# GNN layer, one core: z ahead of n on TensorE and ScalarE, DMA issues apart, edge bias added by VectorE

## The reference

```
h    = relu(layernorm(x))
hid  = relu([h[src], h[dst]] @ W1[t] + b1[t])        # t = type of the edge
m    = hid @ W2[t] + b2[t]
agg  = segment_sum(m, dst)
gi, gh = agg @ W_ih.T + b_ih, h @ W_hh.T + b_hh      # r, z, n parts
r, z = sigmoid(i_r + h_r), sigmoid(i_z + h_z)
n    = tanh(i_n + r * h_n)
out  = x + (1 - z) * n + z * h
```

## Time and profile before

| | |
|---|---|
| median of 3 runs | 1838.65 us (1838.35 to 1839.18) |
| profiled execution | 1840.2 us, its span 1838.3 us |
| TensorE busy | 1667.1 us, 91% |
| VectorE busy | 1595.2 us, 87% |
| ScalarE busy | 1494.6 us, 81% |
| GpSimd busy | 1178.9 us, 64% |
| DMA | 319.72 MB, mean 174 GB/s |

### The profile page before, as it was taken

The page is one execution under the profiler, slowest core; times in us unless marked ns, Lnnn a source line. Parts: engine busy times, 40 slices in busy tenths (PEclk is TensorE's granted clock), DMA queues, the critical chain, the costliest instruction groups (busy, mean ns, idle before and its releaser), DMA issues.

```text
span 1838.3 us, 43100 instructions
## 1 busy us (share of the span) xinstructions
PE 1667.1 (91%) x10182; PEld 1416.6 (77%) x10182; DVE 1595.2 (87%) x4186; ACT 1494.6 (81%) x3401; POOL 1178.9 (64%) x1982
## 2 busy tenths in 40 slices
PE   0226799999999999999999999999999999999998
PEld 0125688888888888888888888888888888888787
DVE  8597798989888988898889888989899989898776
ACT  0025789889888898898888888889898889888795
POOL 5777777776776777777765656666666566666310
PEclk9999899999999999999999999999999999999999
DMA  2225677777777776777677777777777777777653
GB/s 70 51 48 139 168 195 194 192 192 192 198 187 193 191 194 186 187 192 191 187 193 187 190 188 187 187 190 189 189 190 188 190 186 192 189 187 191 161 136 100
DMA packets 477071, 319.72 MB, mean 174 GB/s; under 512 B 106705, under 2 KB 463009, under 8 KB 476962
## 3 DMA queue, kind: packets, MB, share of 16 engines
q10 hardware_dynamic: 261792, 156.12, 28.6%
q1 hardware_dynamic: 185730, 106.99, 25.3%
q0 software_dynamic: 29440, 55.47, 11.8%
HBM read 211.65 MB, written 106.72 MB: 173 GB/s over the span
## 4 chain that ended last, share of the span: by engine, by line
PE 73%; ACT 8%; issue 4%; ACTq 3%; DVE 2%; DMA 0%; SPq 0%; POOL 0%; DVEq 0%; POOLq 0%
PE bank L1329 16%; PE bank L1331 12%; PE bank L1330 12%; PE bank L1409 10%; PE bank L1399 5%; PE bank L1391 5%; PE bank L1421 3%; PE bank L1420 3%; PE bank L1437 3%; ACT n_h L1194 3%; PE bank L1447 3%; ACT n_zc L1282 2%; ACTq L1211 2%; ACT e_r L1270 2%; ACTq L1232 2%
## 5 line engine op out<-in xcount | busy, mean ns | idle before, releaser
L580 POOL DMA_INDIRECT e_x<-in_x,rows_now x816 | 799.6, 980 | 241.7 <-issue 233.4
L1177 ACT ACTIVATE e_h<-e_x,shift,rstd 128x128 f32<-128x128 f32 x816 | 355.3, 493 | 93.6 <-DVE shift L1048 93.6
L1194 ACT ACTIVATE n_h<-n_x,shift,rstd 128x128 f32<-128x128 f32 x784 | 362.8, 489 | 2.1 <-issue 2.1
L1329 PE MATMUL bank<-n_h_hi,whh_hi 128*128 128x512 f32 x588 | 263.0, 447 | 25.3 <-ACT n_zc L1282 18.3
L1113 DVE TENSOR_TENSOR n_d<-bank,n_n 128x512 f32<-128x512 f32 x196 | 135.5, 691 | 160.7 <-ACT n_n L1278 149.1
L1329 PE MATMUL bank<-n_a_hi,wih_hi 128*128 128x512 f32 x588 | 249.3, 424 | 0.9 <-DVE bank L1083 0.9
L1071 DVE TENSOR_SCALAR n_sel<-iota,n_rel 128x256 fp32r<-128x256 f32 x784 | 237.8, 365 | 8.6 <-POOL n_rel L631 7.2
L1409 PE MATMUL bank<-n_sel,n_win 128*128 128x256 f32 x1568 | 234.9, 292 | 8.6 <-DVE n_sel L1071 8.4
L1331 PE MATMUL bank<-n_h_hi,whh_lo 128*128 128x512 f32 x588 | 232.9, 396 | 0.0
L1330 PE MATMUL bank<-n_h_lo,whh_hi 128*128 128x512 f32 x588 | 232.7, 396 | 0.0
L1331 PE MATMUL bank<-n_a_hi,wih_lo 128*128 128x512 f32 x588 | 232.3, 395 | 0.0
(11 more groups left out here) (179 smaller groups left out, 3895.4 us busy)
## 6 DMA issues: line engine op xcount, KB each, us to landing
n_win<-messages SPq DMA_DIRECT2D x1568, 64.2 KB
messages<-e_msg ACTq DMA_DIRECT2D x204, 257.0 KB, 2.7
n_x<-in_x ACTq DMA_DIRECT2D x195, 256.0 KB
out<-n_out ACTq DMA_DIRECT2D x195, 256.0 KB
e_x<-in_x,rows_now POOLq DMA_INDIRECT x816
rows_now<-lists SPq DMA_DIRECT2D x204, 2.0 KB
lists<-picks,list_rows POOLq DMA_INDIRECT x72
w<-in_W SPq DMA_DIRECT2D x1, 512.0 KB, 4.5
```

Of the source, the lines that this page charges most:

```text
L580: G.indirect_dma_start(e_x[:, s, 2 * end + t, :], None, x, bass.IndirectOffsetOnAxis(ap=rows_now[:, s, t, end:end + 1], axis=0)).then_inc( ...
L1177: last = A.activation(e_h[:, s % 2, k, :], e_x[:, s, k, :], ACT.Relu, scale=rstd[:, slot, col + k:col + k + 1], bias=shift[:, slot, col + ...
L1194: last = A.activation(n_h[:, s % 2, cols], n_x[:, s, cols], ACT.Relu, scale=rstd[:, slot, col + 4 + k:col + 5 + k], bias=shift[:, slot, co ...
L1329: T.matmul(o, w_hi, v_hi, start=start, stop=False, skip_group_check=onto)
```

## The change

TensorE makes the z gate ahead of the i_n gate. ScalarE follows: n_zc comes ahead of n_n, and its n_h pieces and DMA issues are put in other places: the store of messages ahead of the last two e_h, one n_h between n_h_hi and n_a_hi, the store of out ahead of an n_h and e_r, the load of x between n_zc and an n_h. The second edge bias is no longer a product of TensorE. VectorE adds it: e_m (SBUF) = messages (PSUM) + b2_all, where b2_all is filled once by ScalarE from a product of TensorE at the start. High and low parts of the messages are then taken from e_m, and TensorE's hidden layer of the next unit waits for e_biased instead of e_low.

```diff
@@ vector, step
                     V.tensor_tensor(e_msg[:, s, :, D:2 * D],
-                                    bank[BE1][:, message_part].rearrange("p (t d) -> p t d", t=2),
+                                    e_m[:].rearrange("p (t d) -> p t d", t=2),
                                     e_msg[:, s, :, 0:D].bitcast(F32), ALU.subtract).then_inc(e_low, 1)
...
                 ln_part(i, m, 5)
+                q = i - 9
+                if within(q, UNITS):
+                    dve.wait_ge(e_messaged, q + 1)
+                    if isinstance(q, int) and q == 0:
+                        dve.wait_ge(b2_copied, 1)
+                    if due(q):
+                        dve.wait_ge(e_low, q)
+                    first = 2 * ((m - 9) % 2)
+                    V.tensor_tensor(e_m[:], bank[BE1][:, message_part], b2_all[:, first * D:(first + 2) * D],
+                                    ALU.add).then_inc(e_biased, 1)
@@ scalar, step
-                normalise_edges(i, m, (0, 1, 2))
+                normalise_edges(i, m, (0, 1))
...
-                normalise_edges(i, m, (3,))
                 store_messages(i, m)
+                normalise_edges(i, m, (2, 3))
...
                     if due(g - 1):
-                        act.wait_ge(n_gate_z, g - 1)
+                        act.wait_ge(n_gate_in, g - 1)
                     A.activation(n_h_hi[:, s, :], bank[BT[s]][:], ACT.Copy).then_inc(n_hhi, 1)
+                normalise_nodes(i, m, (0,))
+                if within(g, NG):
                     act.wait_ge(n_summed, g + 1)
                     A.activation(n_a_hi[:, s, :], bank[BA][:], ACT.Copy).then_inc(n_ahi, 1)
-                normalise_nodes(i, m, (0,))
                 store_out(i, m)
-                load_x(i, m)
+                normalise_nodes(i, m, (1,))
...
-                normalise_nodes(i, m, (1, 2))
...
-                    act.wait_ge(n_gate_in, g + 1)
-                    if due(g - 1):
-                        act.wait_ge(n_ded, g - 1)
-                    A.activation(n_n[:, s, :], bank[BIN][:], ACT.Tanh, bias=bih[:, 2:3]).then_inc(n_ned, 1)
                     act.wait_ge(n_gate_z, g + 1)
                     if due(g - 1):
                         act.wait_ge(n_eed, g - 1)
                     A.activation(n_zc[:, s, :], bank[BRZ][:], ACT.Sigmoid, bias=bneg[:, 1:2],
                                  scale=-1.0).then_inc(n_zed, 1)
+                load_x(i, m)
+                normalise_nodes(i, m, (2,))
+                if within(g, NG):
+                    act.wait_ge(n_gate_in, g + 1)
+                    if due(g - 1):
+                        act.wait_ge(n_ded, g - 1)
+                    A.activation(n_n[:, s, :], bank[BIN][:], ACT.Tanh, bias=bih[:, 2:3]).then_inc(n_ned, 1)
@@ tensor, step
-                        pe.wait_ge(e_low, q)
+                        pe.wait_ge(e_biased, q)
...
+                    pe.wait_ge(n_red, g + 1)
+                    gate(BRZ, 1, s, "ha").then_inc(n_gate_z, 1)
                     pe.wait_ge(n_ted, g + 1)
                     gate(BIN, 2, s, "a", onto=True).then_inc(n_gate_in, 1)
-                    pe.wait_ge(n_red, g + 1)
-                    gate(BRZ, 1, s, "ha").then_inc(n_gate_z, 1)
...
-                    T.matmul(bank[BE1][:, message_part], ones_r[:], b2_rows[:, first * D:(first + 2) * D],
-                             start=True, stop=False)
```

More of the change, by code:

```diff
@@ L131, in gnn_layer @@
         b2_rows = sb("b2_rows", [P, TYPES * D], F32R)
+        b2_all = sb("b2_all", [P, TYPES * D])
+        e_m = sb("e_m", [P, 2 * D])
         row_is = sb("row_is", [P, 2])
@@ L370, in gnn_layer @@
         e_high = sem("e_high")
+        e_biased = sem("e_biased")
+        b2_spread = sem("b2_spread")
+        b2_copied = sem("b2_copied")
         e_low = sem("e_low")
@@ L1271, in step @@
                     last.then_inc(e_relued, 1)
-                normalise_nodes(i, m, (1, 2))
                 g, s = i - LAG, (m - LAG) % 2
+                if within(g, NG):
+                    act.wait_ge(n_gate_z, g + 1)
+                    if due(g - 1):
+                        act.wait_ge(n_eed, g - 1)
+                    A.activation(n_zc[:, s, :], bank[BRZ][:], ACT.Sigmoid, bias=bneg[:, 1:2],
+                                 scale=-1.0).then_inc(n_zed, 1)
+                load_x(i, m)
+                normalise_nodes(i, m, (2,))
                 if within(g, NG):
@@ L1278, in step @@
                     A.activation(n_n[:, s, :], bank[BIN][:], ACT.Tanh, bias=bih[:, 2:3]).then_inc(n_ned, 1)
-                    act.wait_ge(n_gate_z, g + 1)
-                    if due(g - 1):
-                        act.wait_ge(n_eed, g - 1)
-                    A.activation(n_zc[:, s, :], bank[BRZ][:], ACT.Sigmoid, bias=bneg[:, 1:2],
-                                 scale=-1.0).then_inc(n_zed, 1)
                 normalise_nodes(i, m, (3,))
@@ L1286, in step @@
                 if within(q, UNITS):
-                    act.wait_ge(e_messaged, q + 1)
+                    act.wait_ge(e_biased, q + 1)
                     act.wait_ge(e_tagged, q + 1)
-                    A.activation(e_msg[:, s, :, 0:D], bank[BE1][:, message_part].rearrange("p (t d) -> p t d", t=2),
+                    A.activation(e_msg[:, s, :, 0:D], e_m[:].rearrange("p (t d) -> p t d", t=2),
                                  ACT.Copy).then_inc(e_high, 1)
+                if isinstance(i, int) and i == 7:
+                    act.wait_ge(b2_spread, 1)
+                    A.activation(b2_all[:], bank[BIN][:], ACT.Copy).then_inc(b2_copied, 1)
             pipeline(nc, act, LAST, LOOP_END, step)
@@ L1324, in _ @@
             pe.wait_ge(s_gates_ready, 1)
-            T.matmul(bank[BIN][:], ones_r[:], b2_rows[:], start=True, stop=True)
+            T.matmul(bank[BIN][:], ones_r[:], b2_rows[:], start=True, stop=True).then_inc(b2_spread, 1)
             def product(o, w_hi, w_lo, v_hi, v_lo, start, stop, onto):
@@ L1432, in step @@
                     first = 2 * ((m - 9) % 2)
-                    T.matmul(bank[BE1][:, message_part], ones_r[:], b2_rows[:, first * D:(first + 2) * D],
-                             start=True, stop=False)
                     for t in range(2):
                         o = bank[BE1][:, 2 * P + t * D:2 * P + (t + 1) * D]
-                        last = T.matmul(o, e_r[:, s, t * P:(t + 1) * P], w2[:, first + t, :], start=False, stop=t == 1)
+                        last = T.matmul(o, e_r[:, s, t * P:(t + 1) * P], w2[:, first + t, :], start=True, stop=True)
                     last.then_inc(e_messaged, 1)
```

## The result

The changed kernel takes 1976.47 us (median of 4 runs, 1975.02 to 1977.31), the kernel before 1838.5 us; the ratio is 1.075, 95% interval 1.0731 to 1.0768. The forecast was 1979.

What follows compares the result with a forecast made beforehand. TensorE's work and the chain n_n, n_d, n_out, hn bound the step; with n_n later, the loop adds 102 us, the unrolled part 28, other steps 10, together 140, giving 1979 us; whole range 1945 to 2010.

Steps and rivals of the forecast that it cites:

- n_zc at T0-0.51: ScalarE: n_zc starts 0.51 us before T0, the first message product, once z's last product ends at T0-0.53.
- n_zc holds ScalarE 0.57 and the n_h behind it 0.38: ScalarE: these 0.57 and 0.38 us alone would put n_n at T0+0.44 (T0: first message product).
- The load of x 0.13 late in the loop: ScalarE: load between n_zc and n_h starts n_h 0.70 us after n_zc, against 0.57; n_n at T0+0.57 in the loop.
- n_n to hn 2.85: VectorE to TensorE: 2.10 us from n_n to n_out and 0.75 more to hn, so hn at T0+3.42 in the loop.
- hn to T0 5.62: TensorE: from hn to the next first message product 5.60 us, 5.62 with the wait at hn; loop step 9.04.
- r gate was forecast at T0+0.88: TensorE: without the wait for n_zc, r could begin 0.88 us after the first message product.
- 0.08 a step of disturbances carried over: Every step: undisturbed step 8.28 against loop mean 8.36, so 0.08 us was added to each forecast step.
- e_m at 0 by the cover of n_n: VectorE: e_m lets n_d start at T0+0.99, but n_n holds n_d to T0+1.28, so e_m costs 0; cover 0.3 us.
- Its floor: VectorE: if n_n is early, e_m sets n_d at T0+0.99, hn at T0+3.13, step 8.75, 1915 us; chance 4%.
- The store of messages at 0: ScalarE: store now ahead of two e_h, waiting for L1061 to T0+3.7; 0.5 us of slack remains, so cost 0.
- What the change means to save … is worth nothing: ScalarE: e_r's 74.0 us of issue time lies ahead of the 0.5 us slack, so saving it gains nothing.
- A (faster): Rival at hn: early n_n lets TensorE bind, step near 8.0, some 50 us less, 1785; needs n_n at T0-0.11; 5%.

Runs made afterwards that it cites:

- order only: Changed kernel with its new order of TensorE, ScalarE and DMA issues, but the bias kept as TensorE's product with ones, no e_m: 1962.3 us.
- head with ones: Changed kernel, but the first 12 units of edges keep the bias as TensorE's product with ones and have no e_m: 1961.22 us.

## Why the prediction came out

The direction and the mechanism were right. By its steps:

1. *n_zc at T0-0.51*: median T0-0.50 in the loop, with ScalarE idle 0.65 us in front of it. Right.
2. *n_zc holds ScalarE 0.57 and the n_h behind it 0.38*: near enough. n_h to n_n is 0.40 (1000.30 to 1000.70). Before the loop n_n comes at T0+0.47, where 0.44 was forecast.
3. *The load of x 0.13 late in the loop*: the issue came 0.14 behind n_zc, not 0.25, and n_h 0.60 behind it, not 0.70. n_n at T0+0.50, not 0.57. The row used, n_a_hi to the store, has one more n_h between; that this n_h makes the difference is my reading. A term mis-sized by 0.07 us a step. The rule of the Trainium skill (Perfetto Trace Analysis, DVE / Act Engine Instruction), that a waiting compute instruction does not hold the sequencer, has no support in this trace either: the load is issued 0.14 to 0.15 us after n_zc starts in the steps of the loop (0.01 before it), never in the 0.65 us in which n_zc waits.
4. *n_n to hn 2.85*: 2.84 by the medians. *hn to T0 5.62*: 5.62 (1003.58 to 1009.20). Right. So hn is at T0+3.34 instead of 3.42. The r gate was forecast at T0+0.88 and came at 0.80; as hn waits for n_out, that is worth nothing.
5. *0.08 a step of disturbances carried over*: wrong. Median step 8.96, mean 8.98. That ScalarE's 0.65 us of idle time takes up what used to pass through e_r is likely, but no run shows it. With step 3 this makes 8.98 instead of 9.12 in the loop, and 8.96 instead of 8.99 ahead of it; over the 12th to 191st unit +110 where the sum had about +132.
6. *e_m at 0 by the cover of n_n*: right in the loop, shown by order only (8.97) against the changed kernel (8.98). Its floor, n_d at T0+0.99 and a step of 8.75, was measured twice at 8.75. **Wrong in the head**: I looked for its cover in the even steps only. In the first 12 units it cost 14 us, and order the rest of 16.7.
7. *The store of messages at 0*: ScalarE waited 215.9 us in 196 times for the low part, and still came to n_zc early. Right.
8. *"What the change means to save … is worth nothing"*: right for the changed kernel, but read too widely it misleads. In the kernel before that wait was on the path: e_r's issue wait, 74.0 us in the earlier trace rows, was worth 59 us (1842.81 less 1783.67).

So the near agreement, 1979 against 1976.5, is in part luck: a step 0.14 us too long over the 134 steps of the loop and 0.03 over the 42 before it (110 us where the sum had 132) against 16.7 us in the head that the sum did not have. Of the rivals, A (faster) would have needed n_n at T0-0.11; even directly behind n_zc it came at T0+0.20. The 0.96 us of idle time a step left TensorE's granted clock at 1.00 in both windows.

## What to carry to other kernels

In engines that run strictly in order, look for the loop that passes through program order and not only through data: n_n and n_out had nothing to do with each other but their places on VectorE, and 0.8 us on the one was 0.6 us a step on the whole. Before moving an operation forward, ask both who waits for it and what it waits for itself, in the steps at the ends too, where other work is queued behind it. Here two DMA issues in a row on ScalarE held up what came behind them; parting them was worth 3.2% alone, and was lost in a change that put n_n behind n_zc.

## What the runs showed of the hardware that was not expected

The granted clock of the profile is not always TensorE's pace. Between 120 and 160 us it reads 1.00 (2.4 GHz) in the kernel before and 0.50 (1.2 GHz) in the run with the order only. But the same work took the same time in both; the kernel before, then the order only:

```profile
152.73 1.06 PE L1437 MATMUL bank<-w,e_r 128*128 128x128 f32 x4
```

```profile
152.51 1.06 PE L1445 MATMUL bank<-w,e_r 128*128 128x128 f32 x4
```

Four message products take 1.06 us in both heads and 0.61 in the loop, and the product with ones 0.58 in both heads and 0.28 in the loop. So both kernels ran there at the slower pace, whatever the clock reads, and the 1.00 of the earlier trace rows for that stretch, which the expectation of the head with ones took over, is not to be relied on. A clock that reads 1.00 is better checked against the durations of a product that also stands in the loop. What the clock costs in the head no run separates.
